# Attention kernel on Trainium2: the self value products of a head group issued in one stretch instead of four

## Chip, cores and metric

The kernel runs on one core of one Trainium2 chip. The metric is the time of one execution in device microseconds. Clock figures are the granted TensorE clock as the profile gives it, as a share of full speed.

## What is computed

For 16 batches of 512 rows of width 256, the reference does a gated attention block and then a routed feed-forward block. Cut to what matters here (16 heads of depth 16, 64 context rows):

```python
att  = where(causal, q @ k.T / sqrt(16), -inf)      # 512 x 512 per head
attc = qc @ kc.T / sqrt(16)                         # 512 x 64 per head
y    = softmax(att) @ v + softmax(attc) @ vc
x    = x + tanh(g_xattn) * (y @ Wp + bp)
...                                                 # layer norm, top-2 routing, 15 experts, shared expert
```

## The kernel before

The attention part runs over the batches in a software pipeline: `over_batches` calls `body(kind, b)` with the kind "pro", "first" (batch 0), "mid" (14 times), "last" (batch 15) and "post". While batch b is scored, the queries and keys of batch b+1 are projected, and the output of batch b-1 is projected and routed. `PARTS[kind]` says which of these three (prev, cur, nxt) a kind has.

The 16 heads are cut in two chunks c = 0, 1 of 8 heads, each in two head groups g = 0, 1 of 4 heads. In a chunk TensorE walks 24 slots k = 0 to 23, 12 for each group (`GROUP`). Each slot issues one score unit (`score_unit`, L1368): transposed scores for 512 columns into one of three PSUM banks `scalar_bank`. ScalarE takes the exponential of that bank (L869) into `ct` (two cross units X) or `pt` (ten self units A, B, C), and GpSimd zeroes the acausal part of the self tiles (L700, semaphore `masked`). A PSUM bank is free for the score unit three slots later once ScalarE has drained it (`claim_s`).

After the score unit, `beside` adds other work of the slot. Most of it is a maximum unit (`max_unit`, L1402 and L1405; L1398 for the cross ones): scores of the other chunk in one of three banks `vector_bank`, whose negated row maximum VectorE takes (L1199). The same ring of three banks serves the transposed maxima (L1327, copied by L1203), the turned sums (L1347), the value projections (L1314, L1320), the output (L1465, L1474), and the routing transposes and logits (L1442, L1447). A unit waits until VectorE has drained the unit three before it (`claim_v`). The order on VectorE is the order of this ring, with layer-norm and routing steps put between by tables keyed by (c, k): four row normalisations at (0, 14) (L1040), four routing transposes `rT` at (0, 17) to (0, 20), the logits `rl` at (0, 22), which wait until VectorE has copied the last `rT` (L1048), and the steps of the top-2 choice at (1, 0) to (1, 16).

The value products: `pv_cross_products` (L1414) needs the two cross exponentials. `pv_self_products` (L1431) for one key tile kt is four fp32 products, one per head, each of 128 rows onto 32 columns of the array and 32 partitions of the one bank `pv_self`; a head of key tile kt has 512 - 128 kt query columns, so 512, 384, 128 and 256 in the order kt = 0, 1, 3, 2 of `KT_ORDER`. Key tile 0 waits until ScalarE has copied the sums of the group before out of the bank (`pv_drained`, L835), every key tile for its last mask. The stretches of group (c, 0) stand in slots 16, 18, 20 and 22 of its own chunk; those of (0, 1) in slots 1, 3, 5 and 7 of chunk 1; those of (1, 1) all follow each other after slot 23 of chunk 1. ScalarE copies the sums of (c, 0) after the exponential of slot 23, those of (0, 1) after that of (1, 8), and before slot 0 and 12 of a chunk it waits until the products that read the `pt` buffer are done.

Of the kernel before, what the change touches and what calls it, by code (L numbers as in the profile page):

```python
# [82 lines left out]
def attention_phase(nc, x, ctx, g_xattn, W, x1s, g_ffn, router_w, router_bias, turned, rows, keep, ffn, scratch, out):  # L83
# [28 lines left out]
    KT_ORDER = (0, 1, 3, 2)  # L112
# [99 lines left out]
    with ExitStack() as st:  # L212
# [1069 lines left out]
        def _(pe):  # L1282
# [59 lines left out]
            def transpose_sums(kind, b, c, g, w):  # L1342

                ps = claim_v(kind, b, ("tU", c, g, w))
                pe.wait_ge(pv_drained, PV.upto(kind, b, (w, c, g)) if (c, g) != (1, 1) else PV.start(kind, b) - (w == "x"))
                for t in range(QT):
                    last = pe.transpose(ps[:, t * P:(t + 1) * P], usum[w, g][:, t * P:(t + 1) * P], ident[:, :])  # L1347
                last.then_inc(vector_filled, 1)
# [12 lines left out]
            def score_unit(kind, b, c, k):  # L1361

                g, (what, j) = k // len(GROUP), GROUP[k % len(GROUP)]
                ps = claim_s(kind, b, ("st", c, k))
                rows = STACK + MROWS

                def mm(out, head, key0, nk, q0, nq, **kw):
                    return pe.matmul(out, stack[c][0:rows, head, key0:key0 + nk], stack[c][0:rows, head, q0:q0 + nq],  # L1368
                                     start=True, stop=True, **kw)

                h = HEAD_GROUP * g + j
                if what == "X":
                    h = HEAD_GROUP * g + 2 * j
                    for i in range(2):
                        last = mm(ps[i * TC:(i + 1) * TC, :], h + i, KC0, TC, CQ0, T)
                elif what == "A":
                    last = mm(ps[:, :], h, K0, P, Q0, T)
                elif what == "B":
                    mm(ps[:, 0:3 * P], h, K0 + P, P, Q0 + P, 3 * P)
                    last = mm(ps[:, 3 * P:], h, K0 + 3 * P, P, Q0 + 3 * P, P)  # L1380
                else:
                    for i in range(2):
                        last = mm(ps[:, i * 2 * P:(i + 1) * 2 * P], h + i, K0 + 2 * P, P, Q0 + 2 * P, 2 * P)
                last.then_inc(scalar_filled, 1)
# [25 lines left out]
            def pv_cross_products(kind, b, c, g):  # L1410
                pe.wait_ge(pv_drained, PV.upto(kind, b, ("x", c, g)) - 2)
                pe.wait_ge(scalar_drained, SU.upto(kind, b, ("st", c, len(GROUP) * g + 1)))
                for jp in range(2):
                    last = pe.matmul(pv_cross[64 * jp:64 * jp + 64, :], vcst[:, c, 2 * g + jp, :], ct[g][:, jp, :],  # L1414
                                     start=True, stop=True)
                last.then_inc(pv_filled, 1)

            def pv_self_products(kind, b, c, g, kt):
                if kt == 0:
                    pe.wait_ge(pv_drained, PV.upto(kind, b, ("s", c, g)) - 2)  # L1420
                pe.wait_ge(masked, MASKED.upto(kind, b, (c, g, LAST_MASK[kt])))
                for j in range(4):
                    if kt == 0:
                        src = pt[g][:, PT_SLOT[("A", j)], :]
                    elif kt == 1:
                        src = pt[g][:, PT_SLOT[("B", j)], 0:3 * P]
                    elif kt == 3:
                        src = pt[g][:, PT_SLOT[("B", j)], 3 * P:]
                    else:
                        src = pt[g][:, PT_SLOT[("C", j // 2 * 2)], (j % 2) * 2 * P:(j % 2 + 1) * 2 * P]  # L1430
                    last = pe.matmul(pv_self[32 * j:32 * j + 32, kt * P:T], vst[:, kt, c, HEAD_GROUP * g + j, :], src,  # L1431
                                     start=(kt == KT_ORDER[0]), stop=(kt == KT_ORDER[-1]), skip_group_check=True)
                if kt == KT_ORDER[-1]:
                    last.then_inc(pv_filled, 1)
# [43 lines left out]
            def beside(kind, b, c, k):  # L1478
                for name in besides(kind, c, k):
                    if name[0] == "sm":  # L1480
                        max_unit(kind, b, name[1], name[2])
                    elif name[0] == "mT":
                        transpose_max(kind, b, *name[1:])
                    elif name[0] == "tU":
                        transpose_sums(kind, b, *name[1:])
                    elif name[0] == "v":
                        value_products(kind, b, name[1])
                    elif name[0] == "vc":
                        cross_value_products(kind, b, name[1])
                    elif name[0] == "yT":  # L1490
                        transpose_output(kind, b, name[1])
                    elif name[0] == "wp":
                        output_projection(kind, b, name[1])
                    else:
                        route_unit(kind, b, name)

            def shared_units(c, k):

                if (c, k) == (0, 0):
                    pe.wait_ge(scalar_drained, SU.upto("last", LB, ("st", KC - 1, NST - 1)))  # L1500
                    pe.wait_ge(pv_drained, PV.upto("last", LB, ("s", KC - 1, 1)))
                    combine.conv_turned(pe)
                if (c, k) == (0, 3):
                    pe.wait_ge(combine.conv_ready, KC)
                if (c, k) == (0, 8):
                    combine.hole_gate(pe, 0)
                if (c, k) == (0, 23):
                    combine.hole_up(pe, 0)
                    pe.wait_ge(vector_drained, VU.upto("post", B, ("rl",)))
                    combine.hole_up(pe, 1)  # L1510
                if (c, k) == (1, 13):
                    combine.hole_gate(pe, 1)

            def main(kind, b, c):
                prev, cur, nxt = PARTS[kind]
                if cur:
                    pe.wait_ge(m_in[c][0], 16 * (b + 1))
                    pe.wait_ge(vector_drained, VU.start(kind, b))
                for k in range(NST):
                    if cur:  # L1520
                        if k == len(GROUP):
                            pe.wait_ge(m_in[c][1], 16 * (b + 1))
                        score_unit(kind, b, c, k)
                        if c == 1 and k == 0:
                            pv_cross_products(kind, b, 0, 1)
                        if c == 1 and k in (1, 3, 5, 7):
                            pv_self_products(kind, b, 0, 1, KT_ORDER[(k - 1) // 2])
                        if k == 14:
                            pv_cross_products(kind, b, c, 0)
                        if k in (16, 18, 20, 22):  # L1530
                            pv_self_products(kind, b, c, 0, KT_ORDER[(k - 16) // 2])
                    beside(kind, b, c, k)
                    if kind == "post":
                        shared_units(c, k)
                if cur:
                    if c == 1:
                        pv_cross_products(kind, b, 1, 1)
                    transpose_sums(kind, b, c, 0, "x")
                    if c == 1:
                        for kt in KT_ORDER:  # L1540
                            pv_self_products(kind, b, 1, 1, kt)
                    if c == 1 or not nxt:
                        transpose_sums(kind, b, c, 0, "s")
# [786 lines left out]
```

## Time and profile before

| | us |
|---|---|
| time, median of 3 runs | 1625.32 (1623.45 to 1626.36) |
| profiled execution: span from first to last instruction | 1623.5 |
| around that span, against the median | 1.8 |
| attention batches | 16, mid batches 74.0 apart |

The span is 1623.5 us; the median run is 1.8 us more. The pattern of a mid batch repeats every 74.0 us: the `pv_self` stretch that starts at 598.62 in one batch starts at 672.66 in the next. Rows below are of one mid batch unless said otherwise. Start times of an engine's instructions are the reliable measure of its pace: on TensorE durations overlap, so the cost of a piece is taken from its start to the start of the next.

### The profile page before, as it was taken

The page shows a single profiled execution, that of the slowest core. Times are in us where ns is not written, and L with a number is a line of the kernel's source. Part 1 is how long each engine was busy: PE and PEld are TensorE (multiplying, and loading weights), DVE is VectorE, ACT ScalarE, POOL GpSimd, SP SyncE. Part 2 cuts the span into 40 slices and gives each one's busy share as a digit, 9 for nine tenths or more (in the row PEclk, how much of TensorE's full clock was granted, in tenths as well). Part 3 has the DMA queues.
Part 4 walks back from the last instruction along what each step waited for, and adds up shares of the span by engine and source line. Part 5 has one row for each costly group of instructions (what it writes and reads, how often), then busy time and mean ns, then how long its engine had stood idle before and what let it go on. Part 6 is the DMA issues. An engine that isn't in the chain of part 4 may idle for free.

```text
span 1623.5 us, 36170 instructions
## 1 busy us (share of the span) xinstructions
PE 1532.1 (94%) x11348; PEld 941.6 (58%) x11411; DVE 1214.7 (75%) x3093; ACT 882.0 (54%) x1823; POOL 886.2 (55%) x1529
## 2 busy tenths in 40 slices
PE   4899999999999999999999999999997999999696
PEld 2445555555555555555555555555544789998564
DVE  4777787878787777878787877778855566775797
ACT  3365565656655655656566655556460344443555
POOL 2244455564646465555646464655645456776663
PEclk8999999999999999999999999999998999999999
DMA  6754445445454545454454545454464587654897
GB/s 162 197 135 128 140 145 148 147 129 172 137 163 142 151 145 148 133 148 148 143 170 143 144 143 160 139 150 131 142 208 159 161 254 229 176 164 147 262 315 251
DMA packets 185750, 268.32 MB, mean 165 GB/s; under 512 B 26648, under 2 KB 131360, under 8 KB 185568
## 3 DMA queue, kind: packets, MB, share of 16 engines
q1 hardware_dynamic: 149344, 196.34, 43.1%
q0 software_dynamic: 12960, 36.51, 6.1%
q10 hardware_dynamic: 23264, 33.19, 6.0%
q8 instruction: 95, 1.56, 0.4%
q14 instruction: 87, 0.71, 0.2%
HBM read 160.28 MB, written 105.66 MB: 164 GB/s over the span
## 4 chain that ended last, share of the span: by engine, by line
PE 79%; DVE 11%; DMA 3%; ACT 3%; issue 2%; SPq 1%; POOL 1%; DVEq 0%; ACTq 0%; POOLq 0%
PE pv_self L1431 10%; PE scalar_bank L1368 10%; PE scalar_bank L1357 10%; PE vector_bank L1405 7%; PE vector_bank L1901 7%; PE pv_cross L1414 4%; PE vector_bank L1314 4%; PE vector_bank L1402 4%; DVE nmax L1199 4%; PE vector_bank L1474 3%; PE vector_bank L1347 3%; PE vector_bank L1398 2%; PE vector_bank L1447 2%; PE scalar_bank L1888 2%; PE pv_cross L1909 2%
## 5 line engine op out<-in xcount | busy, mean ns | idle before, releaser
L1199 DVE TENSOR_REDUCE nmax<-vector_bank 128x1 f32<-128x384 f32 (+4 forms) x832 | 513.9, 640 | 108.1 <-PE vector_bank L1405 106.7
L869 ACT ACTIVATE pt<-scalar_bank 128x512 f32<-128x512 f32 x640 | 363.4, 598 | 239.7 <-PE scalar_bank L1368 238.0
L700 POOL TENSOR_SCALAR_AFFINE_SELECT pt<-pt 128x256 f32<-128x256 f32 (+1 forms) x640 | 228.0, 367 | 269.1 <-ACT pt L869 262.3
L1368 PE MATMUL scalar_bank<-stack 99*64 99x512 bf16 (+4 forms) x1280 | 294.1, 321 | 1.9 <-DMA stack<-max_scratch 1.0
L1405 PE MATMUL vector_bank<-stack 96*128 96x128 bf16 (+3 forms) x1024 | 248.3, 301 | 3.4
L1357 PE MATMUL scalar_bank<-xnT,w_qk 128*128 128x512 f32 x384 | 182.6, 599 | 1.1 <-ACT xnT L794 1.1
L1735 POOL DMA_INDIRECT rows<-pt x142 | 138.4, 975 | 80.0 <-issue 62.6
L1431 PE MATMUL pv_self<-pt,vst 128*32 128x512 f32 (+3 forms) x2048 | 181.0, 442 | 0.0
L1402 PEld LDWEIGHTS vector_bank<-tri,ident_b 128*128 128x128 bf16 x704 | 68.2, 97 | 190.9 <-DVE nmax L1199 110.3
L1402 PE MATMUL vector_bank<-tri,ident_b 128*128 128x128 bf16 (+2 forms) x641 | 151.8, 237 | 16.1 <-DMA stack<-qk_scratch 10.8
L659 POOL DMA_INDIRECT rows<-xn,slot x128 | 134.1, 1047 | 52.1 <-issue 28.8
L1901 PE MATMUL vector_bank<-pt 128*128 128x128 f32 x1136 | 150.2, 275 | 0.1
L712 POOL TENSOR_TENSOR parts<-q,parts 128x1600 bf16<-128x1600 f32 x30 | 96.8, 3226 | 96.6 <-ACT parts L824 96.3
L1368 PEld LDWEIGHTS scalar_bank<-stack 99*128 99x128 bf16 (+1 forms) x1280 | 102.3, 101 | 70.7 <-issue 23.6
L1901 PEld LDWEIGHTS vector_bank<-pt 128*128 128x128 f32 x1136 | 138.2, 192 | 0.4 <-issue 0.3
L808 ACT ACTIVATE q<-scalar_bank,bias 128x512 f32<-128x512 f32 (+1 forms) x128 | 75.3, 589 | 104.5 <-PE scalar_bank L1357 104.5
L1405 PEld LDWEIGHTS vector_bank<-stack 96*128 96x128 bf16 x1024 | 95.8, 99 | 46.7 <-issue 25.1
L869 ACT ACTIVATE ct<-scalar_bank 128x512 f32<-128x512 f32 x128 | 75.6, 590 | 43.4 <-PE scalar_bank L1368 39.3
L1832 DVE COPY pt<-stack 128x512 f32 x142 | 70.4, 496 | 37.5 <-issue 33.7
L1357 PEld LDWEIGHTS scalar_bank<-xnT,w_qk 128*128 128x128 f32 x384 | 67.8, 191 | 51.0 <-issue 49.1
L1137 DVE TENSOR_TENSOR q<-q,parts 128x512 f32<-128x512 f32 (+1 forms) x128 | 77.1, 603 | 21.1 <-ACT parts L817 17.0
L707 POOL TENSOR_TENSOR y<-y,yc 128x256 f32<-128x256 f32 x64 | 46.2, 722 | 78.4 <-DVE y L1216 78.4
(304 smaller groups left out, 2676.3 us busy)
## 6 DMA issues: line engine op xcount, KB each, us to landing
qk_scratch<-parts SPq DMA_DIRECT2D x31, 1200.0 KB, 4.6
stack<-qk_scratch SPq DMA_DIRECT2D x120, 192.0 KB, 3.0
pt<-rows SPq DMA_DIRECT2D x142, 132.0 KB, 2.4
stack<-qk_scratch SPq DMA_DIRECT2D x248, 72.0 KB, 2.6
pt<-rows SPq DMA_DIRECT2D x16, 1024.0 KB, 6.3
stack<-qk_scratch SPq DMA_DIRECT2D x124, 128.0 KB, 3.1
stack<-qk_scratch SPq DMA_DIRECT2D x240, 36.0 KB, 2.2
xt<-in_x_dram ACTq DMA_DIRECT2D x15, 512.0 KB, 3.9
```

Of the source, the lines that this page charges most:

```text
L659: pool.indirect_dma_start(out=rows[:, :], out_offset=bass.IndirectOffsetOnAxis(ap=slot[:, i:i + 1], axis=0), in_=src[:, i % QT, :], in_off ...
L700: pool.affine_select(out=v, in_=v, compare_op=ALU.is_ge, fill=0.0, base=0, pattern=pat, channel_multiplier=-1).then_inc(masked, 1)
L712: pool.tensor_tensor(parts[:, 2, :], q32[:, :], parts[:, 1, :], ALU.subtract).then_inc(split_done, 1)
L869: act.activation(dst, bank(kind, ("st", c, k))[:, :], ACT.Exp, scale=SCALE).then_inc(scalar_drained, 1)
L1199: dve.tensor_reduce(dst, src, axis=AX, op=ALU.max, negate=True).then_inc(vector_drained, 1)
L1357: last = pe.matmul(ps[:, :], wq[("q", "cq", "k")[i]][:, k, c, :], xnT[:, k, :], start=(k == 0), stop=(k == KC - 1))
L1368: return pe.matmul(out, stack[c][0:rows, head, key0:key0 + nk], stack[c][0:rows, head, q0:q0 + nq], start=True, stop=True, **kw)
L1402: pe.matmul(ps[:, 0:n * w].rearrange("p (h t) -> p h t", t=w)[:, :, qt * P:w], ident_b[:, :], tri[:, 0:n, :], start=True, stop=False, skip ...
L1405: last = pe.matmul(ps[:, i * w:(i + 1) * w], stack[c][0:STACK, h0 + i, qt * P:(qt + 1) * P], stack[c][0:STACK, h0 + i, K0:K0 + w], start=F ...
L1431: last = pe.matmul(pv_self[32 * j:32 * j + 32, kt * P:T], vst[:, kt, c, HEAD_GROUP * g + j, :], src, start=(kt == KT_ORDER[0]), stop=(kt = ...
L1735: pool.indirect_dma_start(out=self.rows[:, :], out_offset=bass.IndirectOffsetOnAxis(ap=self.xg[r][:, self.C:self.C + 1].bitcast(U32), axis=0),
L1901: last = pe.matmul(psGU[q][:, m * P:(m + 1) * P], self.staged[q][:, c, m, :], self.xT[q][:, c, :], start=(c == 0), stop=(c == KC - 1))
```

## The change

The four stretches of a group that stood in four slots stand in one: behind the score unit of slot 20 for group (c, 0), and of slot (1, 5) for group (0, 1). The stretch of four of group (1, 1) stays. Nothing else moves. In a slot the value products stand between the score unit and `beside`.

```diff
@@ main(kind, b, c), in the loop over the slots k @@
                         if c == 1 and k == 0:
                             pv_cross_products(kind, b, 0, 1)
-                        if c == 1 and k in (1, 3, 5, 7):
-                            pv_self_products(kind, b, 0, 1, KT_ORDER[(k - 1) // 2])
                         if k == 14:
                             pv_cross_products(kind, b, c, 0)
-                        if k in (16, 18, 20, 22):
-                            pv_self_products(kind, b, c, 0, KT_ORDER[(k - 16) // 2])
+                        if k == 20 or (c, k) == (1, 5):
+                            g = 0 if k == 20 else 1
+                            for kt in KT_ORDER:
+                                pv_self_products(kind, b, c if g == 0 else 0, g, kt)
                     beside(kind, b, c, k)
```

## Rows read from the trace of the kernel before

**Rows 1.** The page: span, busy time and share of each engine.

```profile
span 1623.5 us, 36170 instructions
PE 1532.1 (94%) x11348; PEld 941.6 (58%) x11411; DVE 1214.7 (75%) x3093; ACT 882.0 (54%) x1823; POOL 886.2 (55%) x1529
```

**Rows 2.** The page: the chain that ended last, by engine.

```profile
PE 79%; DVE 11%; DMA 3%; ACT 3%; issue 2%; SPq 1%; POOL 1%; DVEq 0%; ACTq 0%; POOLq 0%
```

**Rows 3.** Windows: chunk 0, chunk 1 to slot 13, chunk 1 from slot 14.

```profile
656.10:679.50 23.40, 22.70 (x188) 13.01 (x188) 20.35 (x47) 14.12 (x27) 13.67 (x28) 1.00 0.53 145
687.80:703.20 15.40, 14.76 (x143) 8.04 (x143) 13.78 (x51) 10.88 (x23) 6.61 (x11) 1.00 0.44 156
703.20:712.40 9.20, 9.20 (x89) 3.57 (x87) 6.88 (x21) 5.99 (x11) 5.67 (x15) 1.00 0.52 132
```

**Rows 4.** Timeline of PE: group (1, 1) of the batch before, and what follows.

```profile
640.27 2.36 PE L1431 MATMUL pv_self<-pt,vst 128*32 128x512 f32 x32
642.56 0.66 PE L1347 MATMUL vector_bank<-ident,usum 128*128 128x128 f32 x4
```

**Rows 5.** Timeline of PE, chunk 0, slots 16 to 23.

```profile
669.33 0.38 PE L1368 MATMUL scalar_bank<-stack 99*128 99x512 bf16 x1
669.63 1.06 PE L1431 MATMUL pv_self<-pt,vst 128*32 128x512 f32 x8
670.63 0.23 PE L1402 MATMUL vector_bank<-tri,ident_b 128*128 128x128 bf16 x1
...
672.08 0.44 PE L1442 MATMUL vector_bank<-ident,xn 128*128 128x128 f32 x2
...
672.66 0.85 PE L1431 MATMUL pv_self<-pt,vst 128*32 128x384 f32 x8
673.45 0.23 PE L1402 MATMUL vector_bank<-tri,ident_b 128*128 128x128 bf16 x1
...
675.27 0.42 PE L1431 MATMUL pv_self<-pt,vst 128*32 128x128 f32 x8
675.63 0.23 PE L1402 MATMUL vector_bank<-tri,ident_b 128*128 128x128 bf16 x1
...
676.90 0.64 PE L1431 MATMUL pv_self<-pt,vst 128*32 128x256 f32 x8
677.47 0.41 PE L1398 MATMUL vector_bank<-stack 96*128 96x64 bf16 x8
677.71 1.94 PE L1447 MATMUL vector_bank<-router_w,xT 128*128 128x16 f32 x16
```

**Rows 6.** Timeline of DVE, chunk 0, slots 14 to 20.

```profile
669.55 1.53 DVE L1040 TENSOR_SCALAR xn<-xr,mv,rstd 128x256 f32<-128x256 f32 x4
671.01 1.01 DVE L1199 TENSOR_REDUCE nmax<-vector_bank 128x1 f32<-128x384 f32 x2
...
672.27 0.67 DVE L1199 TENSOR_REDUCE nmax<-vector_bank 128x1 f32<-128x512 f32 x1
672.87 0.40 DVE L1048 COPY xT<-vector_bank 128x256 f32<-128x256 f32 x1
673.93 0.69 DVE L1199 TENSOR_REDUCE nmax<-vector_bank 128x1 f32<-128x512 f32 x1 [0.66 <-PE vector_bank L1405]
```

**Rows 7.** Timeline of ACT, chunk 1, the exponential of slot 2.

```profile
691.34 0.60 ACT L869 ACTIVATE pt<-scalar_bank 128x512 f32<-128x512 f32 x1
```

**Rows 8.** Timeline of DVE, chunk 1, slots 5 to 8.

```profile
694.61 0.69 DVE L1199 TENSOR_REDUCE nmax<-vector_bank 128x1 f32<-128x512 f32 x1
...
698.82 0.69 DVE L993 TENSOR_TENSOR vst<-vector_bank,bv 128x512 f32<-128x512 f32 x1 [0.32 <-PE vector_bank L1314]
```

**Rows 9.** Timeline of PE, end of chunk 1.

```profile
712.17 0.41 PE L1398 MATMUL vector_bank<-stack 96*128 96x64 bf16 x8
...
714.32 2.36 PE L1431 MATMUL pv_self<-pt,vst 128*32 128x512 f32 x32
```

**Rows 10.** Timeline of ACT, the last copy of sums of (1, 0) there.

```profile
713.33 0.59 ACT L835 ACTIVATE usum<-pv_self 128x512 f32<-128x512 f32 x1
```

## The prediction

> **What bounds the kernel now.** The page first: TensorE is busy 94% of 1623.5 us, VectorE 75% [rows 1], and the chain that ended last runs over PE for 79% and over DVE for 11% [rows 2]. Time saved on TensorE could thus be time of the kernel, except where VectorE holds it. So the windows by part of a mid batch come next [rows 3]: in the 23.4 us of chunk 0 PE is busy 22.70 and DVE 20.35; in chunk 1 up to slot 13, DVE is busy 13.78 of 15.4; in its last part only 6.88 of 9.2. The change works once in each of these three, and they answer differently, so I walked each through the timelines, slot by slot.
>
> **What the change saves on TensorE.** The instructions are the same, 32 products a group. Their pace, from start to the start of what follows, is 2.29 us for all four key tiles in one stretch (640.27 to 642.56) [rows 4]. Apart they take 1.00, 0.79, 0.36 and 0.57 us, 2.72 in sum [rows 5], so 0.43 less, or 0.14 for each stretch saved. A lone stretch also starts late behind its score unit: 669.33 to 669.63, 0.30 [rows 5]; such a unit takes 0.21 when a maximum unit follows, by my estimate from the neighbouring starts. So 0.09 each, three times 0.27. Together 0.70 us a group, for (0, 1) 0.61, because slot (1, 1) is a cross unit in a narrow tile mode and pays its switch anyway. If TensorE alone set the time, 16 batches would save 16 x 2.0 = 32 us. That is one end.
>
> The joined stretch takes 2.29 us where the lone ones take 2.72, with the same number of products [rows 4, 5]: the overhead goes with the stretch, not with the product. The Trainium skill, TensorEngine Tiling (Array Packing), "Instruction Overhead", gives about 60 cycles to each matmul instead, a cost that would stay with the unchanged count; "Key Properties" of the same page lets each change of tiling mode drain the array, which the rows bear out. By the first the block would cost 2.72 (rival D), by the second 2.29; the sum goes by the rows.
>
> **What it moves.** In slots 16 and 18 the lone stretches gave VectorE time: 1.00 and 0.79 us in which it worked off its three banks. Without them the next maximum units come sooner than VectorE can take them, and then one block of 2.3 us comes in slot 20, ahead of that slot's maximum unit, in which VectorE runs dry. What is lost depends on how full VectorE is there.
>
> *Chunk 0, mid batch.* VectorE does four normalisations from 669.55 and starts the next maximum at 671.01 [rows 6]. Now: slot 16 at 669.33, its maximum unit at 669.55 (not 670.63), transposed maxima, slot 17's score unit by 670.3. The maximum unit of slot 17 needs a bank that VectorE leaves at 671.56 (one 0.47 us maximum and its tail after 671.01): it starts at 671.62, as late as it does now. The routing transpose behind it starts at 672.08, at the end of the pair of maxima (671.01 + 1.01 = 672.02, and 0.06 for the release), exactly as now, and slot 18's score unit 0.27 after it, at 672.35, as now [rows 5, 6]. So the first two things saved, 1.0 us of products and a drain, have bought a wait of one microsecond. From there: maximum unit 672.57; the second transpose waits for the maximum of 672.27 to 672.94 [rows 6], 673.00; slot 19 at 673.27, its maximum unit 673.49; the third transpose waits for the maximum that VectorE takes from 673.20 to 673.87, 673.93; slot 20 at 674.20; the block from 674.51 to 676.80. The maximum unit of slot 20 goes at 676.80, where it went at 675.63 [rows 5]; VectorE starts on it 0.48 later, 677.28, copies the last routing transpose until 678.28 (0.60 + 0.40), and the logits, which need that copy, start at 678.34. They started at 677.71 [rows 5]. TensorE's own work between (0.28 + 0.22 + 0.22 + 0.24 + 0.22 + 0.24) ends at 678.22, under it. So chunk 0 ends 0.63 us *later*.
>
> *Group (0, 1) in chunk 1.* With slots 1 and 3 free, slot 5 waits for the exponential of slot 2, which ends behind other ScalarE work at 691.94 (691.34 + 0.60) [rows 7]; score unit at 692.00, block from 692.31 to 694.60, and the maximum unit of slot 5 behind it. VectorE takes that unit 0.48 later, at 695.08; before it took it at 694.61. It then has no gap before the value copy, which it reached at 698.82 after a wait of 0.32 for TensorE [rows 8]: 698.82 - 694.61 - 0.32 = 3.89 us of work, less 0.08 of the last unit's tail that the next may overlap, 3.81. With the change 695.08 + 3.81 = 698.89, with no wait in it. VectorE then goes on full to slot 13. So 0.07 later, and the 0.61 is gone.
>
> *Group (1, 0).* Here VectorE has slack [rows 3]. Slot 20 starts near 707.95 with one short wait of 0.1, block 708.26 to 710.55, the cross maximum unit of slot 22 at 711.51. It is at 712.17 now [rows 9]: 0.66 earlier. Behind it group (1, 1) needs the bank: TensorE would be there at 714.32 - 0.66 = 713.66 [rows 9]; ScalarE's copy, which ends at 713.92 now (713.33 + 0.59) [rows 10], moves with the exponential of slot 23, which was itself 0.5 us idle for its scores, to some 713.5. It is kept, with 0.15 us to spare.
>
> A mid batch: +0.63 + 0.07 - 0.66 = +0.04 us, 14 of them +0.6. The first batch has no normalisations, no routing and half the VectorE load: all three gains stay, estimated -1.9. In the last batch chunk 1 has no maximum units and ScalarE is the limit: 0.6 lost in chunk 0 as above, and a block of 2.3 us against three banks of 0.55 us each leaves ScalarE dry for some 0.2 to 0.6 us twice; estimated +1.0. Sum: -0.3 us. Against the span 1623.5 that is 1623.2; the median run lies 1.8 above its span, so 1625.0.
>
> What else moves costs nothing: no DMA is issued by these products; the masks they wait for are done earlier than the block; ScalarE's wait for the `pt` buffer at slots 0 and 12 is met sooner (slot 20 instead of 22, slot 5 instead of 7); the bank of sums is written later, so its wait for the copy before is met. Behind the block on TensorE stand the slot's maximum unit and the next score unit; ScalarE has three banks of 0.54 us to live on, and POOL waits with it.
>
> **Rivals.** *A: TensorE alone sets the time* and VectorE's ring takes up the shift. The chain and the 94% speak for it [rows 1, 2], the bank waits in the walk against. It gives 1625 - 32 = 1593. *B: chunk 0's loss is not there*, because VectorE catches up (its gap of 0.66 at 673.93 [rows 6] is what it has to give) or the logits' wait is covered: a mid batch then gains 0.6, 14 x 0.63 = 9 us, 1616. *C, slower: the gain of group (1, 0) is not kept.* ScalarE's copy of the sums of (1, 0) must be over before group (1, 1) starts. It decides from 0.15 us of delay on; with the three score units of slots 21 to 23 inside 1.2 us and three exponentials and a copy at some 0.55 us each behind them, TensorE could wait the whole 0.66. 14 x 0.66 = 9 us, and the same held-up ScalarE in group (0, 1) adds up to 0.1 a batch: 1635. *D, slower: joining saves nothing*, the block costs 2.72 and each start stays as late; 0.43 a block, three blocks, 16 batches: 21 us, 1646. Only a block behind a bf16 score unit that behaves unlike that of group (1, 1), which stands behind transposes [rows 4], would do this.
>
> **How the numbers follow.** My walk: 0.5, with its own range of 0.25 us a batch, 1621 to 1629. B 0.2, A 0.07, C 0.21, D 0.02. A measurement of this kernel tells 0.2% (3.3 us) from no change; the walk's own error reaches over that bound a little on either side, 0.02 to 0.03 each. So faster 0.29, within 0.2% 0.45, slower 0.26. The range from B to C with their errors, 1614 to 1635, leaves out A, D and the tail of C.
>
> **What would show it.** Right if the page has a `pv_self` group with less busy time (about 160 us for 181) and PE less busy in all, but the waits of TensorE for the maxima (L1199) longer by about that, most of it in slots 17 to 19 of chunk 0; if VectorE has an idle gap near 2 us in slot 20 of each chunk; if the logits of chunk 0 start about 0.6 us later against slot 14; if the last part of chunk 1 is 0.66 shorter; and a batch still takes 74.0. Wrong if a joined stretch behind a score unit takes more than 2.3 us, if VectorE is through its units before 671.6, or if TensorE waits for ScalarE's copy before group (1, 1).

## The result: 6 us slower, and the profile after

| | before | after |
|---|---|---|
| median of 5 runs, us | 1624.12 (1623.32 to 1626.36) | 1630.48 (1630.22 to 1633.14) |
| span of the profiled execution, us | 1623.5 | 1630.6 |
| mean granted TensorE clock | 0.983 | 0.979 |

The ratio is 1.0043, with a 95% interval of 1.0031 to 1.0056. The forecast was 1625.0 and no change; the measured time lies in its range, on the side of rival C, but not by C's mechanism.

The page of the changed kernel, the lines that answer to [rows 1, 2], and of its list of groups the one of the value products (engine, mean ns and idle time as before):

```profile
span 1630.6 us, 36233 instructions
PE 1522.1 (93%) x11411; PEld 962.8 (59%) x11411; DVE 1216.3 (75%) x3093; ACT 869.9 (53%) x1823; POOL 887.3 (54%) x1529
...
PE 71%; DVE 14%; ACT 6%; DMA 4%; issue 3%; POOL 1%; SPq 1%; DVEq 0%; ACTq 0%; POOLq 0%
...
L1431 PE MATMUL pv_self<-pt,vst 128*32 128x512 f32 (+3 forms) x2048 | 151.4, 436 | 0.1
```

The products themselves got cheaper, 151.4 us busy where the trace of before has 181.0, and PE is busy 10 us less by the page (rather more in fact, because the page of before has 63 matmul records fewer, all of them missing from its L1402: 641 for 704); yet the span is 7.1 longer. The chain has moved from PE (79 to 71%) to DVE and ACT. The time is waits, or it is a slower clock. TensorE's waits for the maxima (L1402 behind L1199) did grow; the rows are us in total, number of waits and the longest, before and after:

```profile
PE vector_bank L1402 <- DVE nmax L1199: 1.9, 10, 0.3
```

```profile
PE vector_bank L1402 <- DVE nmax L1199: 15.7, 26, 0.9
```

First the pace of a mid batch. The timeline of PE, chunk 0, slots 17 to 23 (compare [rows 5]):

```profile
671.44 0.39 PE L1368 MATMUL scalar_bank<-stack 99*128 99x384 bf16 x2
672.75 0.23 PE L1402 MATMUL vector_bank<-tri,ident_b 128*128 128x128 bf16 x1 [0.92 <-DVE nmax L1199]
...
673.22 0.44 PE L1442 MATMUL vector_bank<-ident,xn 128*128 128x128 f32 x2
...
675.65 2.36 PE L1431 MATMUL pv_self<-pt,vst 128*32 128x512 f32 x32
677.95 0.23 PE L1402 MATMUL vector_bank<-tri,ident_b 128*128 128x128 bf16 x1
...
679.60 1.93 PE L1447 MATMUL vector_bank<-router_w,xT 128*128 128x16 f32 x16
```

And that of DVE there (compare [rows 6]):

```profile
670.69 1.54 DVE L1040 TENSOR_SCALAR xn<-xr,mv,rstd 128x256 f32<-128x256 f32 x4
672.15 1.01 DVE L1199 TENSOR_REDUCE nmax<-vector_bank 128x1 f32<-128x384 f32 x2
...
678.43 0.69 DVE L1199 TENSOR_REDUCE nmax<-vector_bank 128x1 f32<-128x512 f32 x1 [2.16 <-PE vector_bank L1405]
```

The block takes 2.30 us (675.65 to 677.95). The maximum unit of slot 17 waits 0.92 us for VectorE, which has the four normalisations to do first, and VectorE, which was full until the block, is then dry for 2.16 us.

The starts of the `pv_cross` groups (L1414) mark four parts of a batch: chunk 0 from slot 14 to slot 0 of chunk 1; from there to slot 14; to the end of chunk 1; and on to slot 14 of the next batch. Medians over the 14 mid batches, in us (differences of start times that are printed to 0.01 us, so good to about 0.01):

| kernel | chunk 0 | (0, 1) | (1, 0) | rest | batch | mid batches with a clock fall |
|---|---|---|---|---|---|---|
| before | 20.38 | 16.05 | 8.66 | 28.96 | 74.05 | 0 |
| after | 21.13 | 16.10 | 7.94 | 28.96 | 74.13 | 3 |

So at full clock a mid batch went from 74.05 to 74.13 us. That is 1.0 to 1.1 us over 14 of them, and no slowdown to speak of. But three batches took 75.7 to 75.8. In each, the trace shows TensorE at half its clock. The windows around one of them (us, busy of PE, PEld, DVE, ACT and POOL, granted clock, DMA share, GB/s):

```profile
230.60:232.84 2.24, 2.23 (x41) 1.34 (x32) 1.17 (x3) 0.73 (x2) 0.00 (x0) 1.00 0.38 105
232.84:234.70 1.86, 1.86 (x17) 1.86 (x18) 1.71 (x4) 0.36 (x1) 0.70 (x2) 1.00 0.61 171
234.70:238.10 3.40, 3.40 (x10) 2.08 (x9) 1.36 (x5) 1.08 (x2) 1.26 (x5) 0.51 0.64 161
238.10:240.00 1.90, 1.90 (x15) 1.30 (x14) 0.65 (x3) 1.03 (x2) 0.00 (x0) 0.99 0.37 94
```

And the same batch in the kernel before, where the logits start at 233.05:

```profile
233.04:234.90 1.86, 1.86 (x23) 1.86 (x20) 1.28 (x3) 0.00 (x0) 0.41 (x1) 1.00 0.66 187
234.90:238.30 3.40, 3.35 (x21) 2.24 (x22) 1.78 (x7) 1.89 (x4) 1.26 (x5) 1.00 0.71 168
```

The clock is 1.00 (2.4 GHz) while the logits' 16 products of 16 columns run from 232.84, and 0.5 (1.2 GHz) from 234.70 for 3.4 us. A row of PE's timeline in that stretch shows the price:

```profile
235.78 3.07 PE L1357 MATMUL scalar_bank<-xnT,w_qk 128*128 128x512 f32 x4
```

The next piece starts at 238.68, 2.90 us later; the same projection takes 1.72 in the other batches. The page's row of busy shares does not show this: PE is 100% busy in the slow stretch.

**Where 7 us went.** The profiled executions differ by 7.1 us. Term by term, beside what the prediction had for it:

| term of the sum, us | forecast | measured |
|---|---|---|
| first batch | -1.9 | -1.0 |
| 14 mid batches at full clock | +0.6 | +1.0 |
| three clock falls in mid batches (1.62, 1.68, 1.69) | none | +5.0 |
| last batch, to the logits behind it | +1.0 | +2.4 |
| the rest of the kernel | 0 | -0.3 |
| sum | -0.3 | +7.1 |

In the last batch the clock is at half for 6.8 us where it was for 3.4:

```profile
1211.20:1218.00 6.80, 6.80 (x27) 1.74 (x29) 1.44 (x8) 4.58 (x10) 1.80 (x5) 0.52 1.16 302
```

The whole of its chunk 1, from slot 0 to the stretch of group (1, 1), takes 17.94 us before and 20.08 after (length, busy times, clock as above):

```profile
1195.24:1213.19 17.95, 16.87 (x139) 5.79 (x135) 6.73 (x38) 13.84 (x27) 9.73 (x22) 0.95 0.77 221
```

```profile
1200.33:1220.41 20.08, 17.96 (x138) 6.61 (x135) 6.79 (x39) 13.01 (x26) 9.74 (x23) 0.83 0.81 235
```

### The profile page after: what moved, and what is told of

It reads as the page before. It is cut to its first block, busy times and chain, and to the rows that moved or that the text cites. A ratio compares the mean times of both kernels' runs of the same rounds, so it can differ in the third digit from the quotient of the medians.

```text
span 1630.6 us, 36233 instructions
## 1 busy us (share of the span) xinstructions
PE 1522.1 (93%) x11411; PEld 962.8 (59%) x11411; DVE 1216.3 (75%) x3093; ACT 869.9 (53%) x1823; POOL 887.3 (54%) x1529
## 4 chain that ended last, share of the span: by engine, by line
PE 71%; DVE 14%; ACT 6%; DMA 4%; issue 3%; POOL 1%; SPq 1%; DVEq 0%; ACTq 0%; POOLq 0%
PE scalar_bank L1357 10%; PE pv_self L1431 9%; PE scalar_bank L1368 8%; PE vector_bank L1901 6%; PE vector_bank L1405 6%; DVE nmax L1199 4%; PE vector_bank L1314 4%; PE vector_bank L1402 3%; PE vector_bank L1474 3%; PE pv_cross L1414 3%; PE vector_bank L1347 3%; PE vector_bank L1447 2%; ACT q L808 2%; ACT parts L817 2%; PE scalar_bank L1888 2%
## 5 line engine op out<-in xcount | busy, mean ns | idle before, releaser
L1199 DVE TENSOR_REDUCE nmax<-vector_bank 128x1 f32<-128x384 f32 (+4 forms) x832 | 511.1, 638 | 115.8 <-PE vector_bank L1405 114.8
L869 ACT ACTIVATE pt<-scalar_bank 128x512 f32<-128x512 f32 x640 | 358.5, 600 | 255.8 <-PE scalar_bank L1368 254.5
L1368 PE MATMUL scalar_bank<-stack 99*64 99x512 bf16 (+4 forms) x1280 | 290.7, 323 | 4.3 <-DMA stack<-max_scratch 3.1
L1402 PE MATMUL vector_bank<-tri,ident_b 128*128 128x128 bf16 (+2 forms) x704 | 175.3, 249 | 30.0 <-DVE nmax L1199 15.7
L1357 PE MATMUL scalar_bank<-xnT,w_qk 128*128 128x512 f32 x384 | 186.2, 610 | 1.1 <-ACT xnT L794 1.1
L1402 PEld LDWEIGHTS vector_bank<-tri,ident_b 128*128 128x128 bf16 x704 | 68.1, 97 | 166.5 <-DVE nmax L1199 97.8
L1431 PE MATMUL pv_self<-pt,vst 128*32 128x512 f32 (+3 forms) x2048 | 151.4, 436 | 0.1
L1431 PEld LDWEIGHTS pv_self<-pt,vst 128*32 128x32 f32 x2048 | 57.3, 110 | 76.5 <-issue 65.8
```

The costliest lines, as they stand in the source:

```text
L869: act.activation(dst, bank(kind, ("st", c, k))[:, :], ACT.Exp, scale=SCALE).then_inc(scalar_drained, 1)
L1199: dve.tensor_reduce(dst, src, axis=AX, op=ALU.max, negate=True).then_inc(vector_drained, 1)
L1357: last = pe.matmul(ps[:, :], wq[("q", "cq", "k")[i]][:, k, c, :], xnT[:, k, :], start=(k == 0), stop=(k == KC - 1))
L1402: pe.matmul(ps[:, 0:n * w].rearrange("p (h t) -> p h t", t=w)[:, :, qt * P:w], ident_b[:, :], tri[:, 0:n, :], start=True, stop=False, skip ...
```

## Experiments

Theory V after the result: chunk 0 is VectorE's, and the block there costs 0.7 us a batch; the gain of (1, 0) pays that back; and the clock falls come from the order in chunk 0. A mid fall is a stretch of a mid batch with TensorE at half its clock. The rivals: the loss is in (0, 1) or at the end of chunk 1 (W); the block costs its time wherever it stands (P); the falls are chance (N). Ratios are to the kernel before on the same chip, where it took 1625.2 us for the first four kernels, 1626.1 for the next four, 1668.6 for three more and 1667.8 for the last (four chips; the last two are slower, though the attention part of the traces there keeps the same pace; only the ratio is used there).

### One group joined at a time

```diff
 # e1: only (0, 0)            e2: only (1, 0)            e3: only (0, 1)
+if (c, k) == (0, 20):     +if (c, k) == (1, 20):     +if (c, k) == (1, 5):
+    for kt in KT_ORDER:   +    for kt in KT_ORDER:   +    for kt in KT_ORDER:
+        pv_self_products(kind, b, <its chunk>, <its group>, kt)
 # the two other groups in their four slots as before
```

> Only group (0, 0) of chunk 0 is joined, in slot 20; the other groups stay in four stretches. Theory V (VectorE's full ring in chunk 0 and a TensorE that falls to half its clock now and then behind this block): from the pv_cross of chunk 0's slot 14 to that of chunk 1's slot 0 a mid batch takes 21.13 us, as in the changed kernel, for 20.39 before; 14 x 0.74 = 10 us, and clock falls in some mid batches at 1.7 us each, so 1634 to 1641. Rival W (the loss of the whole change lies in the order of group (0, 1) or at the end of chunk 1, where group (1, 1) waits for ScalarE): no slower than before, 1624.

> Only group (1, 0) is joined, in slot 20 of chunk 1. Theory V: the part from slot 14's pv_cross to the end of chunk 1 goes from 8.66 to 7.93 us, all else as before, no clock fall in a mid batch; the last batch gains or loses up to 1: 14 x 0.73 = 10 us, and the first batch 0.7, so 1612 to 1615. Rival W: the 0.73 comes back as a wait for ScalarE before group (1, 1): 1624 or above.

> Only group (0, 1) is joined, in slot 5 of chunk 1. Theory V: 16.10 us for 16.05 from pv_cross to pv_cross, 14 x 0.05 = 0.7 us, plus 0 to 1.7 in the last batch: 1624 to 1627. Rival W: this is where the 6 us went: 1630.

| kernel | chunk 0 | (0, 1) | (1, 0) | batch | falls | median us | ratio (95%) |
|---|---|---|---|---|---|---|---|
| e1, (0, 0) | 21.13 | 16.04 | 8.66 | 74.79 | 2 | 1640.89 | 1.0095 (1.0081 to 1.011) |
| e2, (1, 0) | 20.39 | 16.05 | 7.93 | 73.33 | 0 | 1614.74 | 0.9937 (0.9921 to 0.9953) |
| e3, (0, 1) | 20.39 | 16.10 | 8.65 | 74.10 | 0 | 1626.66 | 1.0007 (0.9995 to 1.0018) |

In the mid batches the three edits act each on its own part and on nothing else, and their effects add up to the changed kernel: +0.75, -0.72 and +0.05 us a mid batch, and for the whole time +0.95, -0.63 and +0.07%, in sum 0.39 for 0.43. W falls: joining (1, 0) keeps its gain whole, and (0, 1) is even there.

The falls of the clock in mid batches come with (0, 0). Two in 14 against none in 14 would be thin evidence by itself, but the mean clock over all runs on this chip says the same: 0.980 for e1 (4 runs) against 0.983 for e2 (6), 0.982 for e3 (11) and 0.983 for the kernel before (23). A stretch of 3.4 us at half clock takes 0.001 off that mean. In e1, windows around one of its two:

```profile
309.00:311.79 2.79, 2.78 (x47) 1.65 (x40) 1.17 (x3) 0.73 (x2) 0.12 (x1) 1.00 0.15 40
311.80:313.60 1.80, 1.80 (x17) 1.80 (x18) 1.69 (x4) 0.35 (x1) 0.70 (x2) 0.99 0.95 245
313.60:317.00 3.40, 3.40 (x11) 2.17 (x11) 1.36 (x5) 1.09 (x2) 1.26 (x5) 0.50 0.41 103
```

Again the logits start at 311.79 and the clock falls 1.8 us later, as they end.

In the last batch (0, 1) is not even. Chunk 1 there takes 20.1 to 22.0 us, with 6.2 to 9.1 of them at half clock, in all six profiled kernels that join (0, 1) (after, e3, e4, e6, e7, e10), and 17.9 to 18.5 us, with 1.8 to 3.7 at half clock, in all eight that leave it in four stretches. Ahead of slot 12 there TensorE waits 1.4 to 2.3 us for the DMA that brings the maxima in (`stack` from `max_scratch`) in each of the six, and 0 to 0.7 us in the eight. So the excess of the last batch goes with the joined (0, 1). Of e3's eleven runs only 1.5 us over before is left in the median; its profiled run is the slowest of them.

### The same block next to the logits

```diff
-if k == 20 or (c, k) == (1, 5):
+if (c, k) in ((0, 22), (1, 5), (1, 20)):   # (0, 0) in slot 22, the others as in the change
```

> The changed kernel with the block of group (0, 0) moved from slot 20 to slot 22, right ahead of the last maximum unit and the logits; the other two blocks as in the changed kernel. By the walk VectorE's bank waits move TensorE to the same start of the logits (678.35 for 678.34), so the pace of a mid batch at full clock should be the same 74.1 us. Theory V says that the clock falls go with the thin work between the block and the logits' end: with the block next to the logits they should go away in the mid batches, 5 us less than the changed kernel, 1624 to 1627, mean clock 0.982 for 0.979. Rival N (the falls have nothing to do with that work, and come by chance or from elsewhere): falls as often as in the changed kernel, 1629 to 1632.

Measured: 1627.33 us, ratio 1.0011 (1.0002 to 1.002), with chunk 0 at 21.11, a mid batch at 74.10, and no fall in any of the 14. PE's timeline there:

```profile
670.71 0.23 PE L1402 MATMUL vector_bank<-tri,ident_b 128*128 128x128 bf16 x1 [0.93 <-DVE nmax L1199]
...
675.00 2.36 PE L1431 MATMUL pv_self<-pt,vst 128*32 128x512 f32 x32
677.29 0.41 PE L1398 MATMUL vector_bank<-stack 96*128 96x64 bf16 x8
677.53 1.94 PE L1447 MATMUL vector_bank<-router_w,xT 128*128 128x16 f32 x16
```

The wait of slot 17 is there (0.93), the pace is the changed kernel's to 0.03 us, and only the thin work between block and logits is gone: 0.24 us of it, for 1.65 in the changed kernel. The mid falls went with it, and 4 to 5 us of the time (4.2 by the medians' distances to their kernels before, 0.3% by the ratios), just over the 1627 that I had put as the upper end. Three falls would be 5.0.

That the clock alone made this difference is likely and not fully shown. The profiled execution of e7 is the slowest of its eleven runs and only 1.8 us shorter than that of the changed kernel: it has 10.2 us at half clock around chunks 0 and 1 of the last batch where the changed kernel has 6.8, and its mean clock is 0.978, not the 0.982 that was expected. Over all runs the mean is 0.981 for e7 and 0.979 for the changed kernel, which is worth about half of the difference. The place of the falls tells the two kernels apart, a single execution's mean clock does not.

### Is it VectorE's backlog?

Two pairs of kernels relieve VectorE in slot 14 of chunk 0, lone stretches against joined ones. e5 and e6 let the four row normalisations work on 16 of 256 columns; e9 and e10 do one of the four. What is left out stays at zero, to which the rows are set once at the start, and the routing then works on rows that are in part zero; only the pace of chunk 0 is read.

```diff
 # e5 (lone), e6 (joined)
-tensor_scalar(xn2[...][:, t, 0:C],  xr[:, t, :],    ...)
+tensor_scalar(xn2[...][:, t, 0:16], xr[:, t, 0:16], ...)
 # e9 (lone), e10 (joined)
-for t in range(QT):
+for t in (QT - 1,):
```

> The kernel before, with VectorE relieved in slot 14 of chunk 0: its four row normalisations work on 16 of 256 columns (the routing then works on rows that are not the reference's; the rest of the rows is set to zero once at the start). About 1.1 us of VectorE work less a mid batch. Theory V: chunk 0 was just about even between the engines, so little comes of it: 20.1 to 20.4 us from pv_cross to pv_cross for 20.38; 1619 to 1625.

> The changed kernel with the same relief of VectorE in slot 14. Theory V: without the backlog the bank wait of slot 17 (0.92 us in the changed kernel) goes, and chunk 0 takes 19.9 to 20.2 us for 21.13, so joining costs nothing there: a mid batch 0.7 to 1.1 us shorter than with lone stretches under the same relief, that is 10 to 15 us less than e5 at full clock. Rival P (the loss in chunk 0 is the block's own, or the late maximum unit of slot 20): chunk 0 still 0.7 longer than in e5, and the two kernels within 2 us.

> The kernel before with one of the four row normalisations of slot 14 and not four (the routing works on rows of which three quarters are zero). Narrow instructions relieved VectorE by 0.37 us only; this takes out a full 1.1. Theory V now says that chunk 0 is VectorE's work plus its gaps, so lone stretches gain until TensorE is the limit: 19.7 to 20.0 us from pv_cross to pv_cross, for 20.38 before and 20.04 with 0.37 relieved.

> The changed kernel with the same 1.1 us of relief. If the backlog of slot 14 is what the loss in chunk 0 comes from, the loss against the lone stretches goes down from 0.7 to about 0 and turns towards the 0.7 saved on TensorE: 19.7 to 20.1 us, no wait in slot 17. If the loss is the gap of VectorE during the block ahead of slot 20's maximum unit, which no relief shortens, chunk 0 stays 0.2 to 0.7 above the lone one: 20.1 to 20.5.

| relief on VectorE | chunk 0, lone | chunk 0, joined | joined less lone | ratios |
|---|---|---|---|---|
| none (before, after) | 20.38 | 21.13 | +0.75 | 1, 1.0043 |
| 0.37 us (e5, e6) | 20.04 | 20.75 | +0.71 | 0.9954, 0.9989 |
| 1.07 us (e9, e10) | 20.04 | 20.07 | +0.03 | 0.996, 0.9903 |

The first pair relieved less than I meant, 0.37 us and not 1.1: a normalisation of 16 columns still takes 0.27. Taken alone it spoke against V, since the loss stayed at 0.71 and e6 came out at 20.75, where 19.9 to 20.2 had been expected. With the second pair the picture is whole. Joined, each microsecond taken from VectorE comes back in full (21.13, 20.75, 20.07), so the joined order is VectorE's down to the last step; lone, 0.34 comes back and then nothing, so from 20.04 on something else is the limit; TensorE, which shows no idle gap between slot 16 and the logits of e9, is the likely one. In e10 the wait of slot 17 is gone while the dry gap in the block stays as it was (DVE, then PE in slot 17):

```profile
664.69 0.47 DVE L1040 TENSOR_SCALAR xn<-xr,mv,rstd 128x256 f32<-128x256 f32 x1
...
671.37 0.69 DVE L1199 TENSOR_REDUCE nmax<-vector_bank 128x1 f32<-128x512 f32 x1 [2.16 <-PE vector_bank L1405]
```

```profile
665.43 0.39 PE L1368 MATMUL scalar_bank<-stack 99*128 99x384 bf16 x2
665.69 0.23 PE L1402 MATMUL vector_bank<-tri,ident_b 128*128 128x128 bf16 x1
```

So the loss takes both: a backlog ahead of the block that makes TensorE wait, and a dry stretch in it that VectorE cannot work ahead for.

### Where the block costs nothing

```diff
 # e4: (0, 0) whole in slot 16, (0, 1) in slot 5, (1, 0) in slot 20
 # e11: the same with (0, 1) in four stretches as before
+if (c, k) in ((0, 16), (1, 20)):
+    for kt in KT_ORDER:
+        pv_self_products(kind, b, c, 0, kt)
 # e8: (0, 0) as pairs, key tiles 0, 1 in slot 16 and 3, 2 in slot 20
 # e12: key tiles 0, 1, 3 in slot 16 and 2 in slot 22
 # e8, e12: (0, 1) in four stretches, (1, 0) in slot 20
```

> The changed kernel with the block of group (0, 0) moved from slot 20 to slot 16, where VectorE has four row normalisations and two maxima to work off (669.55 to 671.94) while TensorE is in the block. Theory V: VectorE is what chunk 0 waits for, so the same block under its backlog costs no bank wait in slot 17: chunk 0 takes about 19.7 us from pv_cross to pv_cross for 21.13, a mid batch 72.7 at full clock. Against it, slots 17 to 22 and the logits are then thin work with no products between, so clock falls of 1.7 us should come at least as often as in the changed kernel (3 in 14); 1604 with none, 1609 with three, 1628 if every mid batch has one. Rival P (a joined block in chunk 0 costs its 0.7 wherever it stands, because any 2.3 us on TensorE lets VectorE run dry): chunk 0 at 21 us, 1625 or above.

> Group (1, 0) joined in slot 20 as in the changed kernel, group (0, 1) in four stretches as before, and group (0, 0) in two pairs: key tiles 0 and 1 in slot 16 (1.64 us), 3 and 2 in slot 20 (0.79 us). Theory V: the pairs are shorter than the work in VectorE's three banks, so VectorE does not run dry, and the two drains saved (2 x 0.23) count at least in part: chunk 0 at 19.9 to 20.4 us, a mid batch 72.9 to 73.3, no clock falls in mid batches since products still stand on either side: 1608 to 1615, no slower than joining (1, 0) alone (1615). Rival P: 0.3 lost in chunk 0, 1619.

> Block of (0, 0) in slot 16, block of (1, 0) in slot 20, group (0, 1) in four stretches as before. Theory V: 19.9 + 16.05 + 7.93 + 28.96 = 72.84 us a mid batch for 72.90 with (0, 1) joined too, and one less heavy load on ScalarE in the last batch, so its end is 0 to 2 us better: 1607 to 1613, the same as or just under the kernel with pairs (1610.8). Clock falls as rare as there (one mid batch in 14).

> Group (1, 0) joined in slot 20, group (0, 1) in four stretches as before, group (0, 0) as key tiles 0, 1 and 3 in slot 16 (under VectorE's backlog) and key tile 2 alone in slot 22, next to the logits, as it stands in the kernel before. Theory V: chunk 0 at 19.9 to 20.0 us for 20.38, so 72.9 us a mid batch, and no clock fall at the end of the logits, since a value product stands within 0.3 us of them, as in every kernel so far without such falls: ratio 0.988 to 0.991. Rival N (falls come by chance when fewer stretches are left): one to three mid batches at 1.7 us more.

| kernel | chunk 0 | batch | mid falls | median us | ratio (95%) |
|---|---|---|---|---|---|
| e4 | 19.90 | 72.90 | 1 | 1613.2 | 0.9915 (0.9894 to 0.9935) |
| e8 | 20.00 | 72.95 | 1 | 1610.75 | 0.9905 (0.9889 to 0.9922) |
| e11 | 19.90 | 72.84 | 2 | 1648.54 | 0.9875 (0.9853 to 0.9896) |
| e12 | 19.99 | 72.93 | 0 | 1649.68 | 0.9892 (0.9874 to 0.991) |

P falls: the same 2.3 us block costs +0.75 us in slots 20 and 22 and gains 0.48 in slot 16. DVE of e4 shows why:

```profile
662.01 1.53 DVE L1040 TENSOR_SCALAR xn<-xr,mv,rstd 128x256 f32<-128x256 f32 x4
663.47 0.54 DVE L1199 TENSOR_REDUCE nmax<-vector_bank 128x1 f32<-128x384 f32 x1
664.82 0.56 DVE L1199 TENSOR_REDUCE nmax<-vector_bank 128x1 f32<-128x384 f32 x1 [0.81 <-PE vector_bank L1405]
```

The block from 662.09 to 664.38 lies over the normalisations, which VectorE had to do anyway, and the dry gap is 0.81 and not 2.16. (I had expected 19.7 us for e4's chunk 0, and 1604 to 1609 us in all.) All four are faster than either kernel of the study, by 0.85 to 1.25%; their intervals overlap, if barely for e4 and e11, and e11 and e12 ran on two other chips, so which is best is open. The falls missed my expectations twice: at least three in e4, which shows one, and none in e8, which shows one too. After e8 I narrowed the theory from "products on either side" to a value product right before the logits.

**The falls, counted.** Each kernel was profiled once, 14 mid batches each. Seven have a value product within 0.3 us of the logits' start (before, e2, e3, e5, e7, e9, e12): 0 falls in 98 mid batches. Seven have their last one 1.65 us before that start or more, with maximum and score units between (after, e1, e4, e6, e8, e10, e11; 5.3 us in e4 and e11): 12 falls in 98, and all 12 begin 1.8 to 2.1 us after the logits' start, none elsewhere in a mid batch. The line between the two groups was drawn after most of the kernels had run; only e12 was built to test it, and by itself it is a weak test, since at one fall in eight batches none in 14 is no surprise. TensorE's wait in slot 17 is not what brings the falls: e7 has it and no fall, e4 and e10 have falls without it. Whether it is the missing value products, the narrow logits or the units between them that count was not taken apart, and why one batch in eight and not each is not settled either.

## Why the prediction was off

**What held.** The walk of a mid batch. Step by step, forecast and measured:

| | forecast | measured |
|---|---|---|
| joined stretch | 2.29 | 2.30 |
| wait of slot 17, bought by the work taken away | about 1 | 0.92 |
| chunk 0 | +0.63 | +0.75 |
| (0, 1) | +0.07 | +0.05 |
| (1, 0) | -0.66 | -0.72 |
| mid batch | +0.04 | +0.08 |

Of the signs it named, the value products are busy 151.4 us (about 160 was said), TensorE's waits for the maxima grew from 1.9 to 15.7 us, and the logits of chunk 0 start 0.75 us later against slot 14. One sign failed: VectorE has no gap near 2 us at the block of chunk 1, but two of 0.62 and 0.64. The gain forecast for (1, 0) was kept; the experiment e2 shows it by itself. The decision for rows against a fixed cost per matmul was right (rival D), and it goes with the Trainium skill, TensorEngine Tiling (Array Packing), "Key Properties": a change of tiling mode drains the array. The trace fits it, since the same 2048 products were busy 30 us less with fewer changes of mode around them; that it is the drain, and nothing else at the start of a stretch, was not tested.

**What failed.** The sum took every step at full clock. "What else moves costs nothing" was written for DMAs, masks, buffers and banks (it held for them in the mid batches); TensorE's own clock was in no term, no rival and no bound, though the profile of before has rows on it. The block took the products away from around the logits and left only maximum and score units, a transpose and 16-column products there. Three falls at 1.6 to 1.7 us are 5.0 of the 7.1 us; with the block next to the logits, at the same pace, e7 has none in a mid batch. The Trainium skill, TensorE: Matmul & The Clock Gate, "Part 1: The HAM clock gate", says that the clock is granted by how busy the array has been of late; that it can fall with PE "busy" at 100% by the profile is what these rows add.

**Two terms mis-sized.** The last batch was put at +1.0 and cost 2.4. Its chunk 1 alone cost 2.1, with 6.8 us at half clock for 1.8; by an estimate, 5 us more at half clock are at most 2.5 us, so the clock could be all of it. But two other things happen there. ScalarE ran dry, as the prediction said and for longer (1.15 us at the first block, where 0.2 to 0.6 was said), and TensorE waited for a DMA of which the prediction had nothing, 1.44 us where it was 0.64; the clock falls 0.6 us after that wait:

```profile
1210.39 0.41 PE L1368 MATMUL scalar_bank<-stack 99*64 99x512 bf16 x2 [1.44 <-DMA stack<-max_scratch]
```

How much of the loss is which stays open; that it goes with the joined (0, 1) is what the fourteen traces above show.

The first batch was put at -1.9 and gave back only 1.0. Its parts take 17.06, 14.32 and 7.93 us for 17.10, 14.64 and 8.66, so in chunk 0, where 0.7 was expected, nothing came. A clock fall lies there in the trace of after, but it is not the whole reason. In e6 the first batch has the same order and no fall in chunk 0: up to the turned sums after slot 23 TensorE is 0.72 us ahead of before, as forecast, and then it stands idle ahead of a maximum unit,

```profile
89.63 0.39 PE L1405 MATMUL vector_bank<-stack 96*128 96x128 bf16 x4 [0.59 <-issue]
```

so that chunk 0 takes 16.90, only 0.2 less than before. What ends that wait the trace does not show.

**The rivals.** A (TensorE alone sets the time) is refuted by e1. B (chunk 0's loss is not there) is refuted by chunk 0 itself; had it held, the time would have been near e2's. C gave the sign, and 10 us where 6 came, by luck: e2 shows that ScalarE's copy holds nobody up. D is refuted by the 2.30. None of the four had the clock in it, so the range held the measured time by luck too.

## What to carry to other kernels

Joining short matmul stretches made them cheaper here (2.30 us for 2.72), but a block in which the consumer of TensorE's other results runs dry is best put over work that the consumer has anyway: the same block cost 0.75 us in slot 20 and gained 0.48 in slot 16. Price a change part by part, the first and the last batch too, and test the parts apart: here a loss, a gain and one part that is even but for the last batch hid in one edit, and the gain alone is 0.6% faster. And when dense products move away from narrow ones, ask what TensorE's clock will do there: the busy share does not show it, the granted clock and a repeated instruction's duration do.

## What the runs showed that I had not expected

- TensorE falls to 1.2 GHz for 3.4 us at the end of 16 products of 16 columns, in 12 of the 98 mid batches of the seven kernels that have no value product right before them, though by the profile it was at work all the time: 1.86 us busy of 1.86 before the fall, and 3.40 of 3.40 in it. Each costs 1.6 to 1.7 us of a 74.1 us batch.
- A VectorE normalisation of 128x16 takes 0.27 us from start to start where one of 128x256 takes 0.365: a sixteenth of the columns gave back only a quarter of the time. (Four of them: 669.55 to 671.01 before, 668.50 to 669.58 in e5.)
